# Summing four expert result rows per token on TensorE instead of VectorE, at two places of a two-layer transformer kernel

## What is computed

```python
x = L0_attn_a_x
x = x + attn_a(layernorm(x))
x = x + ffn(layernorm(x))
x = x + attn_b(layernorm(x))
x = x + ffn(layernorm(x))

def ffn(x):
    scores = softmax(x @ Wg.T)
    # 4 of 16 experts per token, out of the 2 best of 4 groups
    h = silu(einsum('td,eid->eti', x, W1)) * einsum('td,eid->eti', x, W3)
    y = einsum('etd,te->td', einsum('eti,edi->etd', h, W2), combine)
    z = silu(x @ Ws1.T) * (x @ Ws3.T) @ Ws2.T
    return y + z
```

## Time and profile before

| | |
|---|---|
| median of 3 runs | 1328.7 us (1328.54 to 1333.18) |
| the profiled execution's own time | 1329.73 us |
| its span, first to last instruction | 1327.8 us |
| TensorE matmul busy | 1146.8 us, 86% |
| TensorE weight load busy | 614.7 us, 46% |
| VectorE busy | 876.1 us, 66% |
| ScalarE busy | 542.1 us, 41% |
| GpSimd busy | 570.0 us, 43% |
| mean granted TensorE clock | 0.941 of full speed |
| chain that ended last | TensorE 60%, VectorE 21%, ScalarE 6%, issue 6%, DMA 4% |

### The profile page before, as it was taken

How to read it: one execution, slowest core, us unless ns; L and a number is a source line. 1 busy time by engine, 2 the same in 40 slices (tenths; PEclk the granted TensorE clock), 3 DMA queues, 4 the chain that set the end, 5 groups by cost and what they waited for, 6 DMA issues and landing times.

```text
span 1327.8 us, 25926 instructions
## 1 busy us (share of the span) xinstructions
PE 1146.8 (86%) x8708; PEld 614.7 (46%) x8708; DVE 876.1 (66%) x1968; ACT 542.1 (41%) x846; POOL 570.0 (43%) x813
## 2 busy tenths in 40 slices
PE   6887999998889999999377799999878999989990
PEld 2343344443565566555243344444337456655550
DVE  5578989992585344444489799999757744444446
ACT  2124777778531122222132377777865112222210
POOL 4452444544125556433333345554540455563340
PEclk9886999999989999999798899999998998999995
DMA  4522111110643455453554422222026235545528
GB/s 137 156 87 97 40 46 41 48 39 3 255 101 112 146 174 168 140 159 112 200 186 138 150 57 57 57 56 58 15 95 201 75 113 171 177 153 150 148 78 324
DMA packets 105650, 156.67 MB, mean 118 GB/s; under 512 B 19440, under 2 KB 81840, under 8 KB 105008
## 3 DMA queue, kind: packets, MB, share of 16 engines
q1 hardware_dynamic: 91760, 117.53, 29.6%
q0 software_dynamic: 13056, 36.46, 7.6%
q10 hardware_dynamic: 704, 1.02, 0.2%
HBM read 97.76 MB, written 58.58 MB: 118 GB/s over the span
## 4 chain that ended last, share of the span: by engine, by line
PE 60%; DVE 21%; ACT 6%; issue 6%; DMA 4%; POOL 2%; SPq 2%; POOLq 0%; DVEq 0%; ACTq 0%
PE pair_ps L1957 10%; PE o_ps L1721 9%; ACT arena L814 4%; DVE nm L1088 4%; PE pair_ps L1899 4%; PE pair_ps L1990 3%; DVE bm L1088 3%; PE t_ps L1747 2%; PE pair_ps L1671 2%; PE pair_ps L1993 2%; PE pair_ps L1552 2%; PE pair_ps L1651 2%; PE pair_ps L1676 2%; PE pair_ps L1646 2%; PE pair_ps L1944 2%
## 5 line engine op out<-in xcount | busy, mean ns | idle before, releaser
L814 ACT ACTIVATE arena<-pair_ps 128x1024 f32<-128x1024 f32 x320 | 322.7, 1025 | 131.1 <-PE pair_ps L1646 76.3
L616 POOL TENSOR_SCALAR_AFFINE_SELECT arena<-arena 128x512 f32<-128x512 f32 (+1 forms) x320 | 174.9, 547 | 240.9 <-ACT arena L814 240.4
L1088 DVE TENSOR_REDUCE nm<-pair_ps 128x2 f32<-128x1024 f32 (+1 forms) x192 | 232.5, 1221 | 32.9 <-PE pair_ps L1695 29.2
L671 POOL DMA_INDIRECT x_slots<-y_sb,slot_i x128 | 124.0, 969 | 193.8 <-DVE slot_i L1291 89.8
L1721 PE MATMUL o_ps<-arena 128*9 128x512 f32 (+7 forms) x2048 | 177.0, 441 | 4.2 <-POOL arena L616 3.9
L1957 PE MATMUL pair_ps<-arena 128*128 x512 | 170.8, 476 | 1.9 <-ACT arena L865 1.9
L1088 DVE TENSOR_REDUCE bm<-pair_ps 128x8 f32<-128x1024 f32 x128 | 155.2, 1216 | 4.2 <-PE pair_ps L1695 1.0
L1436 DVE TENSOR_TENSOR arena<-arena,pair_ps 128x128 f32<-128x128 f32 x144 | 41.3, 287 | 123.6 <-ACT arena L870 123.2
L1957 PEld LDWEIGHTS pair_ps<-arena 128*128 128x128 f32 x512 | 95.3, 198 | 44.5 <-issue 7.5
L1451 DVE TENSOR_SCALAR xnT<-pair_ps,slot_w 128x256 f32<-128x256 f32 x144 | 65.5, 481 | 73.5 <-PE pair_ps L1995 40.4
L870 ACT ACTIVATE arena<-pair_ps 128x176 f32<-128x176 f32 x144 | 45.7, 317 | 147.0 <-PE pair_ps L1957 130.5
(11 more groups left out here) (282 smaller groups left out, 2005.9 us busy)
## 6 DMA issues: line engine op xcount, KB each, us to landing
arena<-x_slots SPq DMA_DIRECT2D x128, 134.0 KB, 2.2
arena<-in_w SPq DMA_DIRECT2D x4, 2816.0 KB, 18.5
arena<-q_a SPq DMA_DIRECT2D x64, 96.0 KB
arena<-y_f SPq DMA_DIRECT2D x6, 1024.0 KB, 9.9
arena<-q_b SPq DMA_DIRECT2D x64, 96.0 KB
arena<-y_h SPq DMA_DIRECT2D x6, 1024.0 KB, 10.0
arena<-in_w SPq DMA_DIRECT2D x2, 2048.0 KB, 16.9
arena<-in_w SPq DMA_DIRECT2D x72, 48.0 KB, 2.0
```

Of the source, the lines that this page charges most:

```text
L616: pool.affine_select(p, p, pattern, ALU.is_ge, 0.0, base=0, channel_multiplier=-1)\
L671: pool.indirect_dma_start(x_slots, bass.IndirectOffsetOnAxis(ap=slot_i[:, t, k:k + 1], axis=0), y_sb[:, t, :], None).then_inc(sm(f"scat{n ...
L814: act.activation(p_ring[:, U % RING, :], pair_ps[:, pair_at("T", n, u)].rearrange("p a c -> p (a c)"), ACT.Exp, scale=SCALE).then_inc(sm(" ...
L1088: dve.tensor_reduce(dst, src, X, ALU.max, negate=not 2 <= u < 4).then_inc(sm("t_max_done"), 1)
```

## The change

The four rows are summed by TensorE: four products with the identity as the stationary matrix, accumulated in one PSUM bank, `t_ps` for even q and `o_ps` for odd q. VectorE then adds that bank to `x_sb`. This is done for all eight sums of the second layer (h), at the end of the program, and for q = 0 and 1 of the first (f), the first 512 tokens of the second layer's attention. The other six sums of the first layer stay as they were. From q = 2 on, TensorE's products wait until the sum two places before has been added, since its bank is used again.

```diff
+        def sum_ps(q):
+            return (t_ps if q % 2 == 0 else o_ps)[:].rearrange("p (t e) -> p t e", t=2)
+
         def dve_sum(dve, f, q):
             b, u, t = q // 2, q % 2 * 2, 2 * q
-            done = q + 1 + past(f, 2 * B)
+            if f == "h" or q < 2:
+                dve.wait_ge(sm("back_pe"), t + 2 + past(f, TB))
+                dve.tensor_tensor(x_sb[:, t:t + 2, :], x_sb[:, t:t + 2, :], sum_ps(q), ALU.add).then_inc(sm(f + "_x"), 2)
+                return
             part = back[b][:, u:u + 2]
...
-            dve.wait_ge(sm("back_half"), done)
+            dve.wait_ge(sm("back_half"), q - 1)
...
-            dve.wait_ge(sm("back_sum"), done)
+            dve.wait_ge(sm("back_sum"), q - 1)
...
+        def pe_sum(pe, f, q):
+            pe.wait_ge(sm(f"load{q}"), 16 * (loads(q) + past(f, loads(q))))
+            if q >= 2:
+                pe.wait_ge(sm(f + "_x"), 2 * q - 2)
+            rows = back[q // 2][:, q % 2 * 2:q % 2 * 2 + 2]
+            for k in range(TOPK):
+                mm = pe.matmul(sum_ps(q), ident_f, rows[:, :, k, :], start=k == 0, stop=k == TOPK - 1,
+                               skip_group_check=True)
+            mm.then_inc(sm("back_pe"), 2)
...
             pe_ffn(pe, "a", "f")
+            for q in range(2):
+                pe_sum(pe, "f", q)
             pe.wait_ge(sm("b_w"), 112)
             pe_attn(pe, "b")
             pe_ffn(pe, "b", "h")
+            for q in range(2 * B):
+                pe_sum(pe, "h", q)
```

## The result

The changed kernel took 1342.8 us (median of 5 runs, 1336.71 to 1346.08) against 1331.9 us before (5 runs, 1328.54 to 1333.18). The ratio is 1.0102 with a 95% interval of 1.0079 to 1.0125: 13.6 us slower, or 10.5 to 16.7 (the two medians lie 10.9 apart). The profiled execution is the quickest of the five, 1336.71 us with a span of 1334.9.

What follows compares the result with a forecast made beforehand. VectorE was taken to bound the end (DMA only 0.7 us less) and the seam's chain. End 8.83 plus seam 3.35, 12.2 us, on the profiled 1329.7 gave 1341.9, or 1341.0 against the median 1328.7; range 1336.5 to 1346.

Steps and rivals of the forecast that it cites:

- (a): Each sum on TensorE: four float32 identity products take 3.44 us at full clock, 6.88 at half, against VectorE's 2.65.
- the rival at half the price: At both places: an identity product takes one record, a sum 1.72 us; about 1328 in all; chance 0.06.
- (b): Start of both places: TensorE runs 4.4 us at half clock, costing 2.2 us each, with bounds 1.5 and 2.9.
- the bound of 2.9: Start of each place: upper bound, in us, on the cost of TensorE's restart at half clock.
- The rival in which the clock stays at half: Both places: sums stay at half clock, end +34.2 us, seam +8.0, about 1371 in all; chance 0.04.
- (c): End of the program, all eight sums on TensorE: last addition ends 8.83 us later; late loads stay hidden.
- (d): Seam into the second layer's attention: second addition ends 3.35 us later, passed on to all that follows.
- The gain that I allowed for: At the seam: TensorE's next work may run at full clock, at most 2.9 us saved, costed at nothing.
- The additions' price: After each sum on TensorE, VectorE's one addition out of PSUM takes 0.69 us.
- the 80 further records: Sign in the changed kernel's profile: 80 more records of products on TensorE, from 10 sums of 4 products.

Runs made afterwards that it cites:

- e1_seam: Only the two sums at the seam into the second layer's attention go to TensorE, against the kernel before; ratio 1.0014, interval 0.9986 to 1.0042.
- the threefold products: Only the seam's two sums on TensorE, their four products made three times over, against the kernel before; ratio 1.0132, interval 1.0107 to 1.0156.

## Why the prediction was right

1341.0 us was forecast with 1336.5 to 1346.0, and 1342.8 was measured. The forecast was 12.3 us above the three runs shown; the ratio says 13.6. That the number in itself held is in part luck: the kernel before took 1331.9 us beside the changed one, but 1348 to 1353 in three of the later sets, and the same loss on top of that lies outside the range. What the working earned is the loss and where it lies.

(a) The price of a sum was right: 3.43 us measured, 3.44 forecast. The identity product is two records a product like any other, so the rival at half the price was wrong in its premise. Its consequence was right: with half the products the end came to 21.22 us, set by DMA.

(b) The clock: 4.4 us at half were taken for both places, and 4.2 and 3.9 were seen. That they came this close is luck too. In the other traces with all four products once the record of a first sum took 5.44 to 6.74 us, and over all nine such starts it is 1.8 to 3.1 us longer than the 3.60 at full clock, 2.4 in the mean, for the 2.2 of the forecast. The longest, 3.1 us (6.74 - 3.60), is just outside the bound of 2.9 that I had drawn from two restarts. Keeping TensorE at work before the load gave back 1.9 and 2.0 us of the 2.2 forecast. The rival in which the clock stays at half did not occur in any trace: it rose within every first sum of four products.

(c) The end: +8.83 us forecast, +8.72 in the trace. The handover from TensorE to VectorE, which I left out, is 0.10 us (1331.57 to 1331.67), and the shorter time at half clock makes up for it. The late loads were issued at 1311.79, and TensorE never waited for one, as said.

(d) The seam: +3.35 us forecast, +3.41 in the trace. That it goes through in full was argued from a line of VectorE instructions, and is borne out by the threefold products, within 3 us. The gain that I allowed for, TensorE's next work at full clock, did come about only in part: the clock was up at 662.94 and the first transpositions took 0.41 us instead of 0.66, but it fell again within 2 us, and the stretch to the maxima was not shorter.

The additions' price was right: 0.69 us out of PSUM. The profile has the 80 further records that were forecast (8788 for 8708). What the prediction did not foresee is how far two executions of the same code differ: its sum was made against one execution.

## What to carry to other kernels

An idle engine is not a free one: ask what the work costs on it, at the clock that it will have after the idle time, and compare that with the engine that it replaces. Adding four float32 rows by products with the identity costs 0.86 us for each 128x512 piece, while VectorE adds 512 elements in 0.69 and 1024 in 1.22, so it can pay only where VectorE has other work to do at that moment, and no run here shows such a place. At the end of this program the next bound (a load every 2.55 us) is just below the present one (2.65), and a faster way has almost nothing to win.

## What the runs showed of the hardware that I had not expected

- After 10 us without work the time at half clock differed from one execution of the same place to the next: at the seam 4.2 us in the changed kernel and 6.1 us in e1_seam, though both began after 10 us of idle time and worked without a gap. The row in which the clock of e1_seam rises, 671.44, with a first product at 665.30:

```profile
671.00:672.00 1.00, 1.00 (x3) 0.33 (x2) 0.00 (x0) 0.00 (x0) 0.00 (x0) 0.78 1.04 414
```

  The Trainium skill (TensorE: Matmul & The Clock Gate, Part 1: The HAM clock gate) says that the moment of the rise varies from run to run, by 0.5 us either way. That it varies is what these traces show too, but by more: 4.2 and 6.1 us are 2 us apart, and here the measurement decides.
- After 4.05 us without work between the sums and the first transposition, the clock of the changed kernel was still at full, and fell only when TensorE was working again:

```profile
663.00:664.00 1.00, 0.78 (x5) 0.48 (x6) 0.96 (x5) 0.62 (x2) 0.00 (x0) 1.00 1.02 401
664.00:665.00 1.00, 1.00 (x3) 0.80 (x4) 0.97 (x3) 0.04 (x1) 0.00 (x0) 0.56 1.01 410
665.00:666.00 1.00, 1.00 (x5) 0.79 (x4) 0.97 (x2) 0.32 (x2) 0.00 (x0) 0.50 1.05 426
```

  In e1_seam the same code waited 4.04 us, and there the clock fell within the wait (by the row below at 678.26, 1.25 us before the first transposition at 679.51), which then took 0.66 us in place of 0.41:

```profile
678.00:679.00 1.00, 0.00 (x0) 0.00 (x0) 0.83 (x6) 0.00 (x0) 0.00 (x0) 0.63 0.95 340
```

  The stretch from the second addition to attention b's first maxima was 33.18 us there and 33.30 in the changed kernel, so which of the two happens made no difference to it.

- The same code from attention b's first exponentials to the first landing at the end took 548.1 to 564.7 us in the twelve traces, and the kernel before 1331 to 1353 us in different sets of runs. Even between runs that alternate, a difference of 3 us stayed at the edge of the noise (e1_seam, e9_seam); a stretch of the trace shows it at once.
